# The next block's fifth query product stands between the third and the fourth quarter of the output projection instead of behind both

## What is computed

```python
# attention, on q = layernorm(x), k = v = ctx
q1, q2 = split(q @ Wq.T); k1, k2 = split(k @ Wk.T); vh = v @ Wv.T      # 16 heads of 32
w = softmax(q1 k1^T) - lam * softmax(q2 k2^T)
attn = w @ vh
attn = attn * rsqrt(mean(attn*attn) + eps) * g * (1 - LAMBDA_INIT)
x = x + attn @ Wo.T
# feed-forward, on layernorm(x)
h = layer_norm(h, ln1_g, ln1_b)
h = gelu(h @ ternary(w1).T + b1)
h = layer_norm(h, ln2_g, ln2_b)
x = x + h @ ternary(w2).T + b2
```

## Time and profile before

| what | us |
|---|---|
| median of 3 runs | 2377.75 (2376.98 to 2382.32) |
| the profiled execution | 2379.91 |
| its span in the profile | 2377.8 |
| PE busy | 2266.3 (95%) |
| DVE busy | 1693.5 (71%) |
| ACT busy | 1381.4 (58%) |
| POOL busy | 1020.0 (43%) |

### The profile page before, as it was taken

The page is one execution under the profiler, slowest core; times in us unless marked ns, Lnnn a source line. Parts: engine busy times, 40 slices in busy tenths (PEclk is TensorE's granted clock), DMA queues, the critical chain, the costliest instruction groups (busy, mean ns, idle before and its releaser), DMA issues.

```text
span 2377.8 us, 35354 instructions
## 1 busy us (share of the span) xinstructions
PE 2266.3 (95%) x13567; PEld 1058.6 (45%) x13567; DVE 1693.5 (71%) x2659; ACT 1381.4 (58%) x2001; POOL 1020.0 (43%) x807
## 2 busy tenths in 40 slices
PE   8679999999999999999999999999999999999978
PEld 5344534444353444435344444535444453544433
DVE  4667858687685868678686867868576786857673
ACT  3335666566575656657565655656555565655544
POOL 0101625437172543617163462816346281634517
PEclk9779999999999999999999999999999999999999
DMA  7312203131220303122140312213041221302000
GB/s 264 104 45 63 45 24 89 29 83 44 75 52 24 94 24 87 39 67 45 33 104 20 94 33 67 46 51 74 18 106 33 67 46 47 79 20 72 15 23 18
DMA packets 164796, 140.54 MB, mean 59 GB/s; under 512 B 81648, under 2 KB 133420, under 8 KB 164116
## 3 DMA queue, kind: packets, MB, share of 16 engines
q1 hardware_dynamic: 164628, 138.28, 22.2%
HBM read 51.80 MB, written 20.36 MB: 30 GB/s over the span
## 4 chain that ended last, share of the span: by engine, by line
PE 69%; DVE 19%; ACT 4%; SPq 3%; issue 2%; DMA 2%; POOL 1%; POOLq 0%; ACTq 0%; DVEq 0%
PE ps L1471 12%; PE ps L1483 9%; PE ps L1493 6%; PE ps L1321 6%; PE ps L1322 5%; PE ps L1323 5%; DVE arena L1010 5%; PE ps L1416 5%; PE ps L1394 4%; PE ps L1423 4%; DVE arena L1109 4%; PE ps L1369 3%; DVE arena L1003 3%; DVE attn_raw L1048 2%; SPq L470 2%
## 5 line engine op out<-in xcount | busy, mean ns | idle before, releaser
L590 POOL TENSOR_TENSOR attn_raw<-attn_raw 128x512 f32<-128x512 f32 x448 | 612.7, 1387 | 109.6 <-ACT attn_raw L747 102.2
L1471 PE MATMUL ps<-rows,w1T 128*128 128x512 f16 x2048 | 485.4, 380 | 6.6 <-DVE rows L1104 6.6
L1010 DVE TENSOR_REDUCE arena<-ps 128x3 f32<-128x462 f32 (+1 forms) x704 | 412.4, 617 | 89.7 <-PE ps L1369 88.7
L556 POOL TENSOR_TENSOR q<-q 128x512 f16<-128x512 f32 x128 | 151.4, 1188 | 685.0 <-ACT q L693 683.9
L742 ACT ACTIVATE attn_raw<-ps,vec_cols,wstep 128x512 f32<-128x512 f32 x256 | 198.4, 775 | 203.0 <-PE ps L1471 200.4
L1109 DVE SCALAR_TENSOR_TENSOR arena<-attn_raw,vec_cols,arena 128x512 f16<-128x512 f32 x256 | 231.2, 903 | 73.4 <-ACT arena L745 71.6
L1471 PEld LDWEIGHTS ps<-rows,w1T 128*128 128x128 f16 x2048 | 192.5, 98 | 198.2 <-DVE rows L1104 10.2
L1493 PE MATMUL ps<-w2T,arena 128*128 128x512 f16 x1088 | 271.2, 379 | 0.0
L713 ACT ACTIVATE arena<-ps 128x1024 f32<-128x1024 f32 x128 | 131.6, 1028 | 228.4 <-PE ps L1394 228.4
L1030 DVE SCALAR_TENSOR_TENSOR p<-arena,p 128x512 f16<-128x512 f32 x128 | 88.2, 689 | 236.6 <-ACT p L717 236.6
L1369 PE MATMUL ps<-k_att,stack_raw 96*128 96x154 f16 x2048 | 223.0, 234 | 31.8 <-DVE arena L1010 27.4
(11 more groups left out here) (187 smaller groups left out, 3466.9 us busy)
## 6 DMA issues: line engine op xcount, KB each, us to landing
stack_raw<-q SPq DMA_DIRECT2D x768, 64.0 KB, 2.0
arena<-in_x SPq DMA_DIRECT2D x64, 256.0 KB, 2.7
out<-arena SPq DMA_DIRECT2D x64, 256.0 KB, 2.0
arena<-in_x SPq DMA_DIRECT2D x15, 1024.0 KB, 6.9
arena<-in_L_ffn_w SPq DMA_DIRECT2D x7, 1024.0 KB, 10.0
stack_raw<-in_L_xattn_Wq SPq DMA_DIRECT2D x8, 256.0 KB, 5.7
k_att<-k_store SPq DMA_DIRECT2D x4, 490.0 KB
k_store<-attn_raw SPq DMA_DIRECT2D x12, 160.0 KB
```

The source lines that it names most:

```text
L590: ins = pool.tensor_tensor(acc[:, e, :], acc[:, e, :], src[:, j % NG, :], ALU.add)
L1010: dve.tensor_reduce(negmax[:, tt, u0:u1], ps[:, row_bank(c, tb), 0:(u1 - u0) * S].rearrange("p (u s) -> p u s", s=S), AX.X, ALU.max, negat ...
L1471: ins = pe.matmul(ps[:, B_H + j % 2, :], w1T[:, k, j * P:(j + 1) * P], rows16[:, e, k, :], start=(k == 0 and e == 0), stop=(k == KD - 1 an ...
```

## The change

On PE, `queries(i + 1, QATT)`, that is q4, is issued ahead of the fourth quarter of the output projection instead of behind it. q5 and q6 stay where they are. Nothing else is changed.

```diff
                     if tt == TT - 1:
                         wait(pe, s_ol2, i, KD, KD)
                     out_projection(i, tt, (0, 1, 2))
+                if ahead:
+                    queries(i + 1, QATT)
                 out_projection(i, 0, (3,))
                 out_projection(i, 1, (3,))
                 rms_sums(i)
                 out_projection(i, 2, (3,))
                 out_projection(i, 3, (3,))
                 if ahead:
-                    for n in range(QATT, QEARLY):
+                    for n in range(QATT + 1, QEARLY):
                         queries(i + 1, n)
                 h_transposes(i)
```

## The result

| | before | changed |
|---|---|---|
| median | 2377.75 us | 2404.14 us |
| runs | 2376.98 to 2382.32 | 2401.69 to 2404.78 |
| ratio | | 1.0103, 95% interval 1.008 to 1.0126 |
| span of the profile | 2377.8 us | 2399.9 us |
| PE busy | 2266.3 us | 2273.1 us |

The change makes the kernel about 1% slower: by 26.4 us between the medians of three runs, by 24.5 us if the ratio is applied to 2377.75, and by 22.1 us between the two profiled spans. The forecast was 2401.3 us, with a range from 2394 to 2408.

The account below looks back on a forecast made before the run. Two chains bound each block from the row sums to the transposes, PE's query matmuls and DVE's small steps, with 0.42 us of room. Block delays of 25.2 us less 1.7 for the clock gave 2377.75 + 23.5 = 2401.3 us, range 2394 to 2408.

Parts of the forecast that it names:

- Steps 1 and 2: Around the fourth quarter: q4 fills PE's hole of 0.59 us; row sums and DVE's chain behind them move 2.00 us later.
- Step 3: From residual sums to transposes: PE waits 1.2 us for the first residual sums and reaches q7 1.57 us later.
- Step 4: At the hidden product: PE waits for DVE's second low half of h, a delay of 1.75 us.
- Step 5: Hidden product to row maxima: POOL's low half, ACT's q7 copy and first gelu move by 2.00; PE's lateness grows to 2.00.
- Step 6: Sum over blocks: ten normal blocks 20.0, block 0 2.6, block 14 1.6, block 7 1.0, total 25.2 us.
- Step 7: Block 11, hidden product: PE's idle time is split, the clock loss of 1.67 us comes back, leaving 23.5 us.
- The rival in which the clock falls in each block: More idle time drops PE's clock; 11 or so blocks pay 1.67 us more, 2419 us or more; chance 0.10.
- PE's stream is all that counts: Rival: DVE has room for 2 us, so 14 filled holes of 0.59 us give 2369.5 us; chance 0.05.
- The lateness is absorbed: Rival: waits for maxima shrink or DVE and POOL regain half or more of 2.00; 2375 to 2390 us; chance 0.08.

Follow-up runs that it names:

- POOL's step moved: POOL's low half of q5 put ahead of its LN1 power: ratio 1.0004 in the kernel before, 1.0084 in the changed kernel, 0.9982 with 3 q4 matmuls ahead.
- kernels of 3 and 6 matmuls: Only the first 3 or 6 of q4's 12 matmuls put ahead of the fourth quarter, against the kernel before: ratio 0.9997 with 3, 1.0023 with 6.

## Why the prediction was right, step by step

**Steps 1 and 2, the hole and DVE's chain.** Right in mechanism and size: 2.00 us forecast for the row sums, 1.98 to 1.99 measured there, at the residual sums and at the normalised rows.

**Step 3, PE meets DVE.** Right. Forecast were a wait of 1.2 us by issue times for the residual sums (the profile prints 1.12), 9.2 us from the row sums to the transposes (measured 9.16), and q7 1.57 us later (1.52).

**Step 4, the hidden product.** 1.75 forecast, 1.57 measured. I had tied the low halves of h to DVE's own work before them. They start 12.54 us behind the row sums before and 12.33 in every kernel with late sums: before, they were waiting for ACT (0.12 us idle), and DVE had 0.21 us of room that step 4 left out. So q7 ends 1.52 us later and the hidden product starts 0.05 us behind it.

**Step 5, the rest of a block.** The links were right: POOL's low half, ACT's copy of q7, gelu, maxima; moving POOL's step showed it. The size was not: 2.00 forecast, 1.79 measured. q7's copy came 14.79 us behind the row sums in both kernels, a full 2 us later, but gelu stood 16.13 us behind them before and 15.95 now. In the kernel before it waited for the hidden product, not for the copy, and the difference was room. Step 5 had given it none.

**Step 6, the sum.** Between the profiles: the prologue -1.6, block 0 +2.2 (forecast 2.6), the ten normal blocks +18.2 (20.0), block 3 +0.1 (0), block 7 +1.0 (1.0), block 11 -2.3 (0, and -1.7 for the clock), block 14 +3.2 (1.6), block 15 and the end +1.3 (0): 22.1 in all. What hangs on the order of the work are block 0, the ten normal blocks, block 7 and 1.5 us of block 14: 22.9 us, against 25.2 in step 6. Of the 2.2 us too much, 1.8 are the missing room in ten blocks; the rest is block 0, where step 6 charged all of the 2.6 and left out the 0.42 us of room that step 3 has. The other parts (prologue, block 11, the clock, the end) add up to -0.9 and are not shown to come from the change. So the forecast of 23.5 owes some of its closeness to luck: step 7 took off 1.7 us for something that kernels without the new order show as well (below), and that made up for most of the 2.2. Four further runs of the changed kernel gave a ratio of 1.0100, which on 2377.75 is 23.8 us.

**Step 7, the clock.** The number came, but not for the reason given. In block 11 PE no longer stands idle before the hidden product, and its clock stays whole; that block is 2.3 us shorter than before, 1.7 of which is the clock and the rest an earlier DMA. But the new order is not needed for that. With POOL's step moved alone, PE's order is that of the kernel before and its idle time at this place is still in one piece, 1.72 us; the clock stays whole, and block 11 is 2.1 us shorter than in the profile before (PE's timeline, line numbers two higher, and the stretch behind it, to be compared with the earlier trace rows):

```profile
1763.39 1.92 PE L1473 MATMUL ps<-rows,w1T 128*128 128x512 f16 x8 [1.72 <-DVE rows L1106]
...
1763.39:1766.39 3.00, 3.00 (x16) 1.39 (x17) 1.97 (x4) 2.35 (x5) 1.15 (x1) 1.00 0.42 96
```

With q4 behind the row sums it is the same: 1.49 us, a whole clock, 2.35 us shorter. The fall in block 11 belonged to that one execution of the kernel before as much as to its order. The clock also fell elsewhere, which the prediction had named as a sign that it is wrong: in the attention of block 15, behind a wait of 1.70 us that is the same in both kernels. The first fence is the kernel before, the second the changed one; each has the wait in PE's timeline and the busy times of the stretch around it, where the last figure but two is the granted clock.

```profile
2240.64 1.04 PE L1394 MATMUL ps<-stack_raw,k_att 98*128 98x512 f16 x4 [1.70 <-ACT arena L715]
...
2240.00:2260.00 20.00, 19.36 (x118) 6.80 (x119) 11.19 (x14) 11.19 (x13) 0.00 (x0) 1.00 0.11 40
```

```profile
2259.72 1.04 PE L1394 MATMUL ps<-stack_raw,k_att 98*128 98x512 f16 x4 [1.70 <-ACT arena L715]
...
2258.00:2278.00 20.00, 18.30 (x102) 6.21 (x98) 8.45 (x11) 12.27 (x14) 0.00 (x0) 0.91 0.13 40
```

Block 14, counted up to the last low half of block 15, is 3.22 us longer than before in this profile and 3.15 in the second one of the changed kernel, where 1.5 is the delay itself (with q4 before the sums the clock stays whole there, and the block pays 2.11 us for sums 2.59 us late, 0.48 less). The rival in which the clock falls in each block did not come: the ten normal blocks repeat to 0.05 us between the two profiles of the changed kernel, with pauses of 1.12 and 0.44 us in each of them. Here the Trainium skill (TensorE: Matmul & The Clock Gate, "HAM oscillation — how this bites in real kernels") agrees with the rows as to the kind of event, idle gaps followed by the lower level, but not as to "each time", the prediction's words for what the page says of its own case. The wait of 1.70 us stands in all ten profiles, and the clock fell behind it in four (the changed kernel twice, and both kernels with POOL's step moved and q4 or a part of it ahead). What decides it, no row here shows.

**The rivals.** "PE's stream is all that counts" fell with the kernels of 3 and 6 matmuls. "The lateness is absorbed" had a grain of truth, 0.21 us of 2.00; PE's waits at the maxima grew, by 3.2 us in all, and did not shrink.

**One assumption was wrong, with a small effect.** I had taken the DMA behind ACT's copy of q6 in blocks 3, 7 and 11 as fixed in time. In block 3 the copy started 13.95 us behind the last low half before and 12.50 in the changed kernel. Since PE and DVE arrive there 1.6 us later by themselves, that block costs nothing either way. In block 11 it is not so: the copy went from 14.68 to 12.89, and had it stayed, PE would still wait there; 0.7 of the 2.3 us of that block are this. The kernels with late sums share it: over the ten profiles the copy in block 3 starts at 12.49 to 13.14 where the row sums are 2 us late or more, and at 13.95 to 14.84 elsewhere. Why the DMA comes earlier was not tried.

## What to carry to other kernels

Before work is moved into a hole of an engine, look for what another engine awaits behind the hole: here eight small matmuls for the row sums opened a chain of 7.5 us, and putting 2.59 us of work ahead of them to fill 0.59 us cost the difference, less the room at the end of that chain. Fill a hole with no more than it holds, and follow the chain to its end, because the gain stops at the next link with no room (here POOL's low half), and the two edits brought something only together. Where two things end at nearly the same time before a wait, the profile names one; take the gap to the other as room, or a sum over many blocks is off by it.

## What the runs showed that I had not expected

The clock's falls come and go between kernels with the same waits. The kernel before lost 1.67 us at block 11 after an idle time of 2.23 us. The kernel with 3 matmuls ahead fell in blocks 3 and 11 after 2.48 and 2.57 us, and block 3 is 2.2 us longer than before, 1.65 of it from the clock (11.38 us from the hidden product to the maxima instead of 9.73). The kernel with 6 matmuls kept its clock in block 3 after 2.22 us, and the one with 3 and POOL's step moved after 2.23, as long as the wait ahead of the first fall. The changed kernel kept its clock there, and fell in both profiles after 1.70 us in block 15, a wait that left the clock whole in the profile before. A profile's span therefore carries some 2 to 5 us that belong to no edit, which is as much as some of the effects studied here. The lengths of most normal blocks repeat to 0.1 us or better and were the better measure.

The end of the kernel varied too, by up to 3.0 us against the profile before, and most in a kernel with PE's old order (POOL's step moved alone). From the first transpose of block 15 to the second feed-forward product took 12.8 us before and 14.1 in the changed kernel, with the same waits: after the long idle time there PE works at 1.2 GHz, and it came back to 2.4 GHz at different times (mean granted clock of the 10 us from that transpose: 0.80 before, 0.57 changed).

```profile
2303.20:2313.20 10.00, 7.77 (x36) 5.04 (x37) 4.64 (x8) 4.59 (x8) 0.37 (x1) 0.80 0.01 2
```

```profile
2323.90:2333.90 10.00, 7.74 (x29) 4.90 (x30) 4.08 (x7) 3.22 (x6) 0.45 (x1) 0.57 0.01 2
```
